# Moving the squared-K step of the K/V stage from ScalarE to VectorE in an 8-core attention and FFN kernel

## The reference

```python
k = (x @ Wk).reshape(b, s, KVH, DH)      # KVH = 4, DH = 128
v = (x @ Wv).reshape(b, s, KVH, DH)
k = _rmsnorm(k, k_gamma)                 # t * rsqrt(mean(t*t) + EPS) * gamma
scores = einsum('bqhd,bkhd->bhqk', q, k) * DH ** (-0.5)   # causal, softmax, @ v, @ Wo, + x
```

## Time and profile before

| | us |
|---|---|
| median of three runs | 6487.2 |
| lowest and highest of the three | 6400.19 and 6504.29 |
| the profiled execution | 6178.7 |
| span of its slowest core (core 0) | 6177.0 |
| spans of all 8 cores | 6156.2 to 6177.0 |
| granted TensorE clock, mean, all cores | 0.830 to 0.833 |
| stage one, K and V | 0 to 722 |

### The profile page before, as it was taken

One profiled execution on the slowest core, in us unless ns is written; L12 is line 12 of the kernel. 1 busy time (PEld: TensorE's weight loads), 2 busy tenths in 40 slices (PEclk: granted clock), 3 DMA queues, 4 the chain that ended last, 5 costly groups with the idle time before them and its releaser, 6 DMA issues.

```text
span 6177.0 us, 56292 instructions; the slowest of 8 cores (6156.2 to 6177.0 us)
## 1 busy us (share of the span) xinstructions
PE 4318.0 (70%) x16064; PEld 1553.4 (25%) x16384; DVE 1702.8 (28%) x3262; ACT 1491.4 (24%) x2179; POOL 294.2 (5%) x231
## 2 busy tenths in 40 slices
PE   4554445564666546666467666489999879999998
PEld 1211111111111111111111111134444334444443
DVE  3555343333333333332323233321111211111000
ACT  2011223302444035552056655001010000001000
POOL 0000000010000100000000000100000100001000
PEclk9766656685767768888788888789999989999999
DMA  4111223071221711203510200855658994565797
GB/s 96 58 62 62 45 36 48 23 116 28 36 30 28 102 28 25 34 14 55 80 26 18 31 13 12 110 67 37 41 35 64 105 96 41 36 41 35 52 79 70
DMA packets 692807, 311.33 MB, mean 50 GB/s; under 512 B 543870, under 2 KB 614526, under 8 KB 692510
## 3 DMA queue, kind: packets, MB, share of 16 engines
q0 software_dynamic: 598576, 147.86, 32.5%
q1 hardware_dynamic: 93934, 159.85, 9.4%
HBM read 572.62 MB, written 33.88 MB: 98 GB/s over the span
## 4 chain that ended last, share of the span: by engine, by line
PE 53%; DVE 15%; ACT 14%; DMA 8%; issue 7%; DVEq 1%; SPq 1%; ACTq 1%; another core or an unknown queue 0%; POOLq 0%
PE ps L112 41%; PE lacc L112 12%; ACT pbt L124 10%; DVE xnn L132 3%; DVE pbt L132 3%; ACT rowb L124 3%; DVE rowb L132 2%; DMA dbuf<-dw 2%; DMA wofc<-wo 2%; DVE xtmp L132 1%; DVE rlB L132 1%; ACT rlrow L124 1%; DMA rbc<-rlrow 1%; DMA rlB<-rbc 1%; DMA x1t<-rbc 1%
## 5 line engine op out<-in xcount | busy, mean ns | idle before, releaser
L124 ACT ACTIVATE pbt<-ps,biasB,rall 128x512 bf16<-128x512 f32 x1280 | 995.7, 778 | 740.9 <-PE ps L112 349.4
L112 PE MATMUL ps<-pbt,vtok 128*128 128x512 bf16 x1255 | 581.3, 463 | 614.7 <-ACT pbt L124 296.3
L112 PE MATMUL lacc<-fuse,dbuf 128*128 128x512 bf16 x3010 | 692.6, 390 | 104.5 <-DMA dbuf<-dw 50.4
L112 PE MATMUL ps<-xn,gbuf 128*128 128x512 bf16 x3012 | 695.1, 381 | 77.8 <-DVE xn L132 74.4
L112 PE MATMUL ps<-xn,ubuf 128*128 128x512 bf16 x3010 | 689.8, 379 | 3.2
L112 PE MATMUL ps<-qhat,khat 128*128 128x512 bf16 x1239 | 583.6, 475 | 27.5 <-DVE qhat L132 22.8
L124 ACT ACTIVATE gact<-ps,gs_sb 128x512 bf16<-128x512 f32 x192 | 132.0, 688 | 1623.7 <-PE ps L112 1580.1
L132 DVE SCALAR_TENSOR_TENSOR fuse<-ps,us_sb,gact 128x512 bf16<-128x512 f32 x192 | 144.2, 751 | 1178.0 <-PE ps L112 1128.6
L112 PEld LDWEIGHTS lacc<-fuse,dbuf 128*128 128x128 fp8e4 x3072 | 305.2, 100 | 491.9 <-issue 153.1
L132 DVE TENSOR_TENSOR pbt<-pbt 128x512 bf16<-128x512 bf16 x640 | 272.2, 425 | 545.0 <-ACT pbt L124 512.0
L112 PEld LDWEIGHTS ps<-xn,gbuf 128*128 128x128 fp8e4 x3072 | 301.7, 98 | 441.3 <-issue 82.1
(11 more groups left out here) (83 smaller groups left out, 2431.3 us busy)
## 6 DMA issues: line engine op xcount, KB each, us to landing
xtt<-xT SPq DMA_DIRECT2D x128, 256.0 KB, 2.8
wqhg<-wq POOLq DMA_DIRECT2D x32, 1024.0 KB, 11.0
wofc<-wo POOLq DMA_DIRECT2D x64, 512.0 KB, 9.2
gbuf<-gw POOLq DMA_DIRECT2D x48, 512.0 KB, 9.2
ubuf<-uw POOLq DMA_DIRECT2D x48, 512.0 KB, 13.4
dbuf<-dw POOLq DMA_DIRECT2D x32, 768.0 KB, 22.2
xtt<-xq SPq DMA_DIRECT2D x64, 256.0 KB, 8.1
x1t<-rbc SPq DMA_DIRECT2D x64, 256.0 KB, 3.2
```

The lines of the kernel that those rows point to most:

```text
L112: eng.matmul(o, l, r, start=st, stop=sp))
L124: eng.activation(out=o, in_=i, func=f, **kw).then_inc(sem["S"], 1))
```

## The change

In the K statistics loop the PSUM copy and the square go from ScalarE's stream to VectorE's: a `tensor_copy` for the Copy activation, a `tensor_tensor` multiply for the Square activation. The waits in front of them and the wait of TensorE behind them change their engine or counter with them. Nothing else in the stream is moved, so on VectorE the pair of a head stands behind the previous head's `khat` and, for head 1, behind `p1_rows`.

```diff
                         b = KB[kvh]
-                        wait("scalar", "T", t_kp[kvh])
-                        gwait("scalar", gd.get("ksq"))
-                        act(ktmp[:, :], ps[b][:, :], AF.Copy)
-                        s_ksq = act(ksq[:, :], ktmp[:, :], AF.Square, inc=True)
-                        wait("tensor", "S", s_ksq)
+                        wait("vector", "T", t_kp[kvh])
+                        gwait("vector", gd.get("ksq"))
+                        vop("tensor_copy", ktmp[:, :], ps[b][:, :])
+                        s_ksq = vop("tensor_tensor", ksq[:, :], ktmp[:, :], ktmp[:, :],
+                                    ALU.mult, inc=True)
+                        wait("tensor", "V", s_ksq)
                         wait("tensor", "V", v_vc_last)
                         gwait("tensor", gd.get("kstatbank"))
```

## The result

The change makes the kernel slower by 0.67%: the ratio of the changed kernel's time to that of the kernel before, taken over like executions, is 1.0067, with a 95% interval of 1.0036 to 1.0098. On the 6178 us of the profiled execution that is 41 us (22 to 61). The profiled execution of the changed kernel took 6225.84 us.

A forecast was written before the change was run, and what follows sets the result against it. It took a ring of three engines (DVE, ACT, PE) with no slack at each tile's end as the bound. Loop 44.6 us plus clock 6.3 made about 51, added to the median: 6538 us, +0.8%, range 6440 to 6590.

The forecast's parts named there:

- I add the 51 us to the median: Whole kernel: the 51 us sum added to the median of three runs, giving 6538 us, +0.8%.
- this possibility in its last sentence: Whole kernel: a median far from 6538 with stage one grown 45 to 51 us would mean the difference between executions decides.
- The sum for the loop: K statistics loop, stage one: seven tiles at 5.45 us, 38.2, plus 6.4 in tile 7, makes 44.6 us.
- Head 0: First sums of a tile: PE starts 1.68 us after `vtok` instead of 0.25, +1.43 us.
- Head 1: Its pair waits on DVE behind `p1_rows`, so PE starts at 229.07 instead of 228.31, +0.76 us.
- Heads 2 and 3: Their pairs start behind `khat`, so PE's step grows from 3.28 to 4.91 us, +1.63 each.
- The hop from VectorE's square to PE: End of the square to PE's start: taken as 0.36 us; 0.25 would take off 3.5 us in all.
- Tile 7: Last tile, without `p1_rows`: all three steps grow to 4.91 us, 1.43 + 3 x 1.65 = 6.4 us.
- The clock term: Longer PE gap before `sq_mms`, about 2.6 us: 1.69 us lost in 8 of 15 tiles, 6.3 us in all.
- the pair hides by itself: Rival: DVE runs the next head's pair in its idle before `nbt`; 9 us less, 6478 us; chance 0.06.
- nothing moves: Rival: the next tile waits for something later than `khat`, which swallows the shift; 6487 us; chance 0.05.
- the clock stays down through the dense part: Rival: PE stays at 1.2 GHz through the next tile's K and V products; 215 us more, 6753 us; chance 0.04.

The follow-up runs named there:

- The doubled pair: Changed kernel with head 0's copy and square done twice on VectorE: loop 227.3 us, 23.4 more than the changed kernel; all 56 groups long.
- the square alone: Kernel before with only the square moved to VectorE, the copy staying on ScalarE: loop 178.2 us on cores 0, 1, 6 and 7, +19.1.
- the two doublings: Changed kernel with head 0's copy and square done twice (loop 227.3 us), or only its copy done twice (39 of 56 groups long).
- the best place: Kernel before with pairs moved early, behind the K products, in four `ksq` buffers: loop 130.8 us on ScalarE, 130.7 us on VectorE.
- head 0 alone: Kernel before with only head 0's copy and square moved to VectorE, heads 1 to 3 staying on ScalarE: loop 170.8 us, +11.7.
- pair before `khat`: Changed kernel with the next head's copy and square placed before this head's `khat` on VectorE: loop 173.0 us, +13.9 against the kernel before.
- pair before `nbt`: Changed kernel with the next head's copy and square before `nbt` on VectorE, two `ksq` buffers: loop 156.2 us, -2.9 against the kernel before.

## Why the prediction was right or wrong

**The time: wrong, below the range.** 6538 us with 6440 to 6590 was given, 6360.28 was measured. The step that failed is the last of the sum, "I add the 51 us to the median", with its range from the three runs (lowest plus 41, highest plus 70): it took 6487.2 us as the time that the change is added to. The profiled execution stood 308 us under that median, the prediction said that it had no row for the difference, and then left the one execution that it could read out of the range. In 16 runs the kernel before had a median of 6425.43 us: five took 6178 to 6192 us and the other eleven 6380 to 6548, so the three shown were all from the upper group. Of the changed kernel's 16 runs seven took 6203 to 6261 us and nine 6346 to 6628. So the median fell by 65 us, while like executions were 41 us longer: it goes by how many runs were short, and not by the edit. The prediction named this possibility in its last sentence, but gave it no room in its range. A range from 6178.7 + 41 to 6504 + 70 would have held it, by its width. The change itself was forecast at +0.8% and measured at +0.67% (0.36 to 0.98%); that it would stay within 2% was right.

**The sum for the loop: right, with two small errors against each other.** 44.6 us against 44.9, of which 0.4 are the two long groups. Head 0: +1.43 predicted, 1.69 - 0.25 = 1.44 measured. Head 1: +0.76, and 11.28 - 10.52 = 0.76. Heads 2 and 3: 4.91 and 4.91. The hop from VectorE's square to PE, taken at 0.36 from ACT's row rather than 0.25, was 0.36 (235.10 to 235.46); only in tile 0 it was 0.26 and in tile 7 0.45. Tile 7 was a little off, with +6.1 us for the 6.4 in the sum (13.76 to 19.81), and small delays of some 0.3 us in single steps, in both kernels, make up the difference. By the table of the Trainium skill (VectorE: DVE Perf Modes, the section on the TRN2 errata) an estimate of the pair is 0.99 us. The rows say 0.692 + 0.426 = 1.12, and the measurement decides.

**The clock term: the mechanism exists, the size was wrong.** 6.3 us were taken, from gaps of 2.06 us in the FFN where 8 of 15 bursts were long. Two of 56 groups were long in the changed kernel, 1.34 and 1.69 us, so 0.4 us a core. The doubled pair shows that the cost is there once the gap is 3.9 us, at the 1.69 us predicted for each. What failed was to carry a chance from one place to another by the length of the gap alone. The 15 bursts gave a warning: the first eleven alternate, long and short, with ten of the eleven gaps at 2.06 or 2.07 us, so they were no even chance by the gap. This term moved the forecast by 6 us and is not why the time fell out of the range.

**What the sum left out** went the other way. The dense part was 1.8 us shorter (492.4 to 490.6) and the first tile began 1.9 us earlier in the mean of the cores (71.7 to 69.8). Neither is edited; the dense part moved between 489 and 496 us in all the kernels on cores with the usual clock, and the start of the first tile between 67 and 73 us. No run shows a cause for either. Stage one: 44.9 - 1.8 - 1.9 = 41.2, and it ended 41.1 later. The sum with the clock term said 51, without it 45.

**Did it reach the end?** In part. The mean span of the cores less the end of stage one was 5444 us before, 5427 in the changed kernel, and 5425 to 5453 in seven other kernels (all but the square alone and the two doublings, which had long stretches at a granted clock of 0.81). The later stages scatter by 14 us either way, without order by kernel. In the profiles alone the mean span grew by 24 us and the slowest core's by 47. The ratio over many runs, 22 to 61 us, speaks of the slowest core and fits the 41 us of stage one. The mean over the eight cores grew less: it was 6194 us in the eight executions of the changed kernel that took under 6261 us, and 6174 us in the eleven of the kernel before that took 6173 to 6236 us, which were measured beside other runs. That is 20 us for a stage one that ends 41 us later. Whether the later stages give back the rest, and why, stays open.

**The rivals.** That the pair hides by itself fell, as its condition said: it hides only when it stands before `nbt` in the stream, and then it does, with 2.97 us a step (2.73 was worked out, without VectorE's own 2.97 us of work and the gaps between its operations). That nothing moves fell: the next tile's `xtmp` still follows `khat` after 0.10 us, 5.4 us later in the tile. That the clock stays down through the dense part fell: it was 490.6 us, against 492.4.

## What to carry to other kernels

When work moves to another engine, price first what stands ahead of it in that engine's stream and only then its duration: here the same 1.12 us of work changed the loop by +45, +14, -3 and -28 us over 32 passes, by its place (and the buffers of `ksq` that the last two places were given), and at the best place the engine made no difference. An engine's idle time counts for nothing unless the moved work is issued in front of the wait that makes it. And where executions of one kernel fall into groups, forecast a ratio of like executions and let the range in microseconds cover every group that is in hand, the profiled execution's among them.

## What the runs showed of the hardware

How often TensorE's clock falls behind a gap does not go by the gap's length alone. The gap from the V products to the first sums, and the long groups after it, each kernel in one execution:

| gap us | kernel | long groups |
|---|---|---|
| 1.12 | before | 0 of 56 |
| 1.76 | square alone, cores 0, 1, 6, 7 | 0 of 28 |
| 2.55 | changed | 2 of 56 |
| 2.55 | head 0 alone | 4 of 56 |
| 2.55 | pair before `khat` | 10 of 56 |
| 2.55 | pair before `nbt` | 16 of 56 |
| 3.35 | copy of head 0 doubled, cores with the usual clock | 25 of 42 |
| 3.88 | pair of head 0 doubled | 56 of 56 |

The four kernels with a gap of 2.55 us have the same V products ahead of it and differ in the length of a tile. In the FFN of the kernel before, 8 of 15 bursts were long at a gap of 2.06 us, and they did not fall at random: the first eleven alternate, long and short. Both fit a rule in which the gap's place in time counts too; which rule, was not tried here.

A third granted clock, 0.81, showed on pairs of cores in four of the thirteen profiles. In the kernel with the square alone moved, cores 2 to 5 had it in stage one: `sq_mms` groups took 4.36 us where the usual is 3.61, and the dense parts 533 us instead of 492. A window over one such group on core 2 (stretch, length, busy, granted clock, DMA share, GB/s):

```profile
326.33:330.69 4.36, 4.36 (x19) 0.81 0.00 0
```

The other three are the pair before `khat` and the two kernels that double work of head 0, there on cores 2 and 3 in stage one. The nine others, the kernel before and the changed one among them, have none of it. What brings it is not shown.
